# Token lists of a routed expert layer: 64 one-hot steps against four chunks of 16

## The chip, the cores and the metric

The kernel is one program on one core of a Trainium2 chip. The metric is the device time in microseconds. The engines are TensorE (matrix products, with a weight load ahead of each), VectorE, ScalarE, GpSimd (which here issues gathers and scatters by index) and SyncE (which issues plain transfers). They run side by side and meet at semaphores.

## The reference, cut to what matters

The reference is a four-layer network on 16 images of 64 channels and 16 x 16 positions, 4096 tokens. Each layer is a mixing block and a mixture of 8 experts, of which each token uses two. The change lies in the experts of the first layer:

```python
t = _to_tokens(x)                              # [16, 256, 64]: 4096 tokens
t = t + _L0_ffn_ref(_ln_t(t), L0_ffn_router_w, L0_ffn_w1, L0_ffn_w2, L0_ffn_w3)
# router -> softmax -> the best two of 8 experts, weights divided by their sum
# each expert: (silu(x @ w1) * (x @ w3)) @ w2, hidden width 682
```

This kernel computes that layer only for the experts a token has chosen: 8192 pairs of token and expert are sorted by expert, padded to whole blocks, and each block of 256 slots is computed with one expert's weights.

## The kernel before

All of it is in `routed_experts()`. A token is (partition p, turn t): p from 0 to 127, t from 0 to 31. With two choices k, a pair has the number n = 32 k + t on its partition, 0 to 63. The sort has these steps, one behind the other.

1. Preparation. The tokens are normalised (VectorE, ScalarE, and GpSimd for the power), split in a high and a low half-precision part `xs`, stored to memory as rows, turned by TensorE, and multiplied by the router's weights. Beside this ScalarE copies the ramp 0 to 127 to half precision (`iota16`, L1546), computes `row_code` = 1 + p/1024 (L1547), and the first two chunks of expert weights are split, the high half by ScalarE (`split_high`, L1449), the low half by VectorE (`split_low`, L1455).
2. Positions. VectorE finds the best two experts, counts, and gives each pair a slot. A slot is a column (0 to 77, 39 blocks of two half blocks) and a row (0 to 127): `col` and `row` (L1730, L1731).
3. Token lists. They invert the map: for slot (row r, column c), which token is it? For each n of 64, VectorE makes two one-hot arrays (L1740, L1742): `hot_slot[p, r]`, which has a code at r = row, and `hot_col[p, c]`, which has `row_code` at c = col. TensorE multiplies them (L1844) and adds all 64 in one bank. There are four buffers of each, so VectorE may be four steps ahead. As each slot has at most one pair, a sum holds one number, the product of `(1 + (n % 4) / 4) * 2 ** (n // 4)` and 1 + p/1024.
4. Owner. Three VectorE instructions (L1744 to L1747) compute which expert each of the 39 blocks belongs to.
5. Decode. 20 VectorE instructions (L1752 to L1773) take n and p out of the number's bits, and write `take` (the token's row, to be gathered) and `give` (the pair's row, to be scattered). The last raises the semaphore to LISTED.
6. GpSimd issues gathers (L1622), two for each block and seven blocks ahead, as soon as LISTED is there, and later scatters (L1630). VectorE meanwhile computes the gates (L1777 to L1788) and two low weight halves; the loads of the next weight chunks on SyncE (L1444) wait for these.
7. 39 blocks. TensorE turns the gathered rows (L1855), ScalarE copies them (L1574), TensorE multiplies (L1871), ScalarE applies Silu (L1566), VectorE multiplies (L1798, L1802), TensorE multiplies by w2 (L1881), ScalarE copies the rows out.

Each engine has its instructions in the order in which the code is written; there is no scheduler. `c.link` makes an instruction wait for the one before it on its engine. A tile's name in the profile may carry the suffix `_stage`.

## Time and profile before

| | us |
|---|---|
| device time, median of 3 runs | 1105.27 |
| lowest and highest | 1104.97, 1107.36 |
| profiled execution: first to last instruction (span) | 1104.3 |
| TensorE busy | 864.2 (78%) |
| VectorE busy | 735.0 (67%) |
| ScalarE busy | 629.9 (57%) |
| GpSimd busy | 285.6 (26%) |

Of the profiled execution the span is what is on record, with no separate device time. The busy shares are averages over stages with quite different limits. The sort and the first layer's experts lie between 117 and 410 us. A row of the timeline gives the start, the duration, the engine, the line, the operation, what it writes and reads, the number of elements per partition, and in brackets the idle time ahead of it and who ended it.

### The profile page before, as it was taken

Reading aid. Unit: us, or ns where it says so; the run is one execution under the profiler, and the core shown is the slowest. Engines: PE = TensorE matmul, PEld = TensorE weight load, DVE = VectorE, ACT = ScalarE, POOL = GpSimd, SP = SyncE. Lnnn points to the kernel's source line nnn. Section 1 sums busy time; section 2 is a strip of 40 time slices with the busy share of each in tenths; the row PEclk is TensorE's granted clock in tenths of the full one; section 3 lists DMA queues with packets and bytes.
Section 4 is the critical chain, followed back from the end, with each engine's and each line's share of the span. In section 5 each row is a group of like instructions: output and inputs, shape, how many; then the busy total and the mean of one; then the engine's idle time right before and its main releaser. Section 6 shows DMA issues by size and latency. Waiting matters only on the chain. (4 is left out here: it accounts for less than half of the span.)

```text
span 1104.3 us, 21444 instructions
## 1 busy us (share of the span) xinstructions
PE 864.2 (78%) x6822; PEld 579.7 (52%) x6822; DVE 735.0 (67%) x1964; ACT 629.9 (57%) x1293; POOL 285.6 (26%) x313
## 2 busy tenths in 40 slices
PE   4877134999999916678888867996877999958597
PEld 2665112999999915556666643443443444425232
DVE  7677788664444446878888877887585445445775
ACT  5553300654444435588888845885655777746353
POOL 3012302777777714400000002112130010025100
PEclk9889555999999966579999987997797999989699
DMA  4000271330000020101111100000100000000000
GB/s 129 1 0 0 51 132 31 93 88 20 23 22 25 19 91 1 39 30 58 38 57 38 48 20 1 1 1 21 38 1 1 1 0 0 1 12 10 1 1 38
DMA packets 25270, 32.66 MB, mean 30 GB/s; under 512 B 11582, under 2 KB 14665, under 8 KB 24814
## 3 DMA queue, kind: packets, MB, share of 16 engines
q1 hardware_dynamic: 20206, 27.50, 8.8%
q0 software_dynamic: 4992, 4.22, 1.5%
q8 instruction: 43, 0.70, 0.3%
q14 instruction: 29, 0.24, 0.1%
HBM read 19.31 MB, written 4.91 MB: 22 GB/s over the span
## 5 line engine op out<-in xcount | busy, mean ns | idle before, releaser
L1798 DVE SCALAR_TENSOR_TENSOR routed_hid_stage<-ps,routed_act_stage 128x512 f32<-128x512 f32 (+1 forms) x117 | 70.6, 604 | 100.1 <-ACT routed_act_stage L1566 98.7
L1566 ACT ACTIVATE routed_act_stage<-ps 128x512 f32<-128x512 f32 x117 | 69.9, 598 | 87.2 <-PE ps L1871 86.0
L1881 PE MATMUL ps<-w_sb,routed_hid_stage 128*128 x936 | 117.6, 269 | 0.0
L1128 ACT ACTIVATE hid_stage<-ps,b_col_sb 128x512 f32<-128x512 f32 x192 | 116.0, 698 | 0.0
L1871 PE MATMUL ps<-routed_x_stage,w_sb 128*128 128x256 f16 x858 | 114.9, 276 | 0.8 <-ACT routed_x_stage L1574 0.8
L1881 PEld LDWEIGHTS ps<-w_sb,routed_hid_stage 128*128 128x128 f32 x936 | 113.6, 192 | 1.5
L412 POOL TENSOR_TENSOR st_sb<-st_sb,neg_half_sb 128x4 f32 (+1 forms) x32 | 37.5, 1173 | 252.8 <-DVE st_sb L407 252.8
L1622 POOL DMA_INDIRECT routed_got_stage<-expert_rows,take_stage x78 | 81.6, 1047 | 78.1 <-DVE give_stage L1773 54.6
L1079 PE MATMUL ps<-x_sb,w_sb 128*128 (+1 forms) x384 | 94.5, 388 | 2.8 <-ACT hid_stage L1128 2.8
L1093 PE MATMUL ps<-hid_stage,w_sb 128*64 128x512 f32 x384 | 93.5, 606 | 1.3 <-DVE gated_stage L1160 1.3
L1871 PEld LDWEIGHTS ps<-routed_x_stage,w_sb 128*128 x858 | 84.3, 104 | 9.4 <-issue 1.1
L1160 DVE TENSOR_TENSOR gated_stage<-ps,rt_sb 128x512 f32<-128x512 f32 x64 | 44.2, 691 | 64.0 <-PE ps L1102 63.0
L1630 POOL DMA_INDIRECT expert_out<-routed_rows_stage,give_stage x78 | 79.4, 1018 | 23.8 <-issue 22.9
L322 POOL TENSOR_TENSOR st_sb<-st_sb,neg_half_sb 128x16 f32<-128x16 f32 x6 | 17.3, 2907 | 229.1 <-DVE st_sb L256 229.1
L1079 PEld LDWEIGHTS ps<-x_sb,w_sb 128*128 128x128 f16 x384 | 33.7, 99 | 76.7 <-issue 26.8
L1135 ACT ACTIVATE y_sb_stage<-ps,b_col_sb 128x512 f32<-128x512 f32 x64 | 43.4, 693 | 37.2 <-PE ps L1093 37.2
L2325 DVE CUSTOM_DVE_ANT_0 sq_sb<-ps,rel_bias_sb 128x256 f32<-128x256 f32 x128 | 47.6, 420 | 16.8 <-PE ps L2223 14.5
L1167 DVE TENSOR_TENSOR x_tok_sb<-x_tok_sb,gated_stage 128x256 f32<-128x256 f32 (+1 forms) x128 | 54.4, 425 | 5.7
L2301 ACT ACTIVATE sq_sb<-sq_sb,nmax_stage 128x256 f32<-128x256 f32 x128 | 56.0, 501 | 0.5 <-DVE nmax_stage L2325 0.3
L2325 DVE CUSTOM_DVE_ANT_0 xn_tok_sb<-ps,rel_bias_sb 128x256 f32<-128x256 f32 x128 | 47.6, 420 | 12.5 <-PE ps L2223 10.6
L2301 ACT ACTIVATE xn_tok_sb<-xn_tok_sb,nmax_stage 128x256 f32<-128x256 f32 x128 | 54.6, 500 | 0.0
L348 PE MATMUL ps<-idn_sb,xn_tok_sb 128*64 128x128 f32 x96 | 17.9, 373 | 46.8 <-DVE xn_tok_sb L264 46.8
(404 smaller groups left out, 1861.9 us busy)
## 6 DMA issues: line engine op xcount, KB each, us to landing
w_stage_sb<-f_w SPq DMA_DIRECT2D x32, 176.0 KB
x_sb<-w_sb SPq DMA_DIRECT2D x16, 256.0 KB, 2.4
rt_sb<-vals_stage SPq DMA_DIRECT2D x16, 256.0 KB, 2.3
rel_bias_sb<-bias_bands SPq DMA_DIRECT2D x16, 128.0 KB
w_stage_sb<-f_w SPq DMA_DIRECT2D x14, 128.0 KB, 3.0
w_sb<-f_w SPq DMA_DIRECT2D x1, 1536.0 KB
routed_got_stage<-expert_rows,take_stage POOLq DMA_INDIRECT x78, 2.5
expert_out<-routed_rows_stage,give_stage POOLq DMA_INDIRECT x78, 2.2
```

The source lines that it names most:

```text
L1079: last = nc.tensor.matmul(ps[:, n % BATCH, :], w16[:, part, col:col + P], xg, start=(part == 0), stop=(part == 1))
L1093: last = nc.tensor.matmul(ps[half * C:(half + 1) * C, bank, :], w2[:, at_w2:at_w2 + C], hid[:, n % RING, :], start=(m == 0), stop=(m == TP ...
L1128: nc.scalar.activation(hid[:, n % RING, :], ps[:, n % BATCH, :], func, bias=b1_col[:, b:b + 1], scale=UNSCALE).then_inc(h_act, 1)
L1167: nc.vector.tensor_tensor(xg, xg, gated[:, :, half, :], ALU.add).then_inc(added, 1)
L1566: nc.scalar.activation(act_h[:, n, :], ps[:, H1 + (q + n) % 2, :], ACT.Silu, scale=UNSCALE).then_inc(h_act, 1)
L1622: nc.gpsimd.indirect_dma_start(out=got[:, b % GOT, h, :], out_offset=None, in_=rows_d[:, :], in_offset=bass.IndirectOffsetOnAxis(ap=take[: ...
L1630: nc.gpsimd.indirect_dma_start(out=slots_d[:, :], out_offset=bass.IndirectOffsetOnAxis(ap=give[:, 2 * b + h:2 * b + h + 1], axis=0), in_=y ...
L1798: last = nc.vector.scalar_tensor_tensor(hid[:, q % 2, n, 0:full], ps[:, H3 + (q + n) % 2, 0:full], UNSCALE, act_h[:, n, 0:full], ALU.mult, ...
L1871: last = nc.tensor.matmul(o, w16[:, part, bass.ds(col, P)], xb[:, q % 2, :], start=(part == 0), stop=(part == 1))
L1881: last = nc.tensor.matmul(ps[:, Y + q % 2, h * C:(h + 1) * C], hid[:, q % 2, n, a * BLK + h * P:a * BLK + (h + 1) * P], w2[:, bass.ds(e * ...
L2301: last = nc.scalar.activation(prob[k % RING][:, a, :], prob[k % RING][:, a, :], ACT.Exp, bias=nmax[:, k % RING, a:a + 1], scale=-1.0)
L2325: last = nc.vector.tensor_tensor_reduce(out=prob[k % RING][:, a, :], in0=ps[:, k % SB, a * N:(a + 1) * N], in1=rel_bias[:, nt, hp + 4 * a, ...
```

## The change

The pairs are handled in four chunks of 16 instead of one by one.

- `iota16` now has each number of the ramp 16 times side by side, 2048 elements (L1553 of the changed kernel). `row_code` is gone; `turn16` holds n + 1 in half precision (L1554). Column and row are written in half precision, which adds one conversion (L1742) ahead of the lists.
- For a chunk VectorE compares the whole ramp with 16 columns at once (L1755, 78 x 16 = 1248 elements, equality, no code), then with 16 rows (L1757, 128 x 16 = 2048), and multiplies the column flags by n + 1 (L1760, 1248). ScalarE multiplies the column flags by the partition's number p (L1568).
- TensorE's 64 products (L1848) have 156 columns: 78 for the sum of p and 78 for the sum of n + 1. Each reads its operands at a step of 16 elements, since the 16 pairs of a chunk lie innermost. The buffers are two deep and lie in tiles that are free at that time (`sq`, `routed_act`, `routed_hid`).
- The decode needs no bits taken apart: 7 instructions in place of 20 (L1765 to L1771). The three owner instructions stand behind it (L1773 to L1776), and TensorE waits for them before the first block's turn; GpSimd waits for the decode as before.
- Some loads in this and later stages share counters (`const`, `maps`).

```diff
-            iota16 = sbl("sort_iota16", [P, P], F16)
+            LIST_CHUNKS = 4
+            PER_CHUNK = TOPK * NT // LIST_CHUNKS
+            iota16 = sbl("sort_iota16", [P, P, PER_CHUNK], F16)
+            turn16 = sbl("sort_turn16", [P, TOPK * NT], F16)
+            row16 = sbl("sort_row16", [P, TOPK * NT], F16)
+            col16 = sbl("sort_col16", [P, TOPK * NT], F16)
...
-            hot_slot = sbl("hot_slot", [P, 4, P], F16)
-            hot_col = sbl("hot_col", [P, 4, COLS0], F16)
-            row_code = sbl("sort_row_code", [P, 1])
...
+            hot_slot = sq[:, :, :].rearrange("p t c -> p (t c)").bitcast(F16).rearrange(
+                "p (q r n) -> p q r n", q=2, n=PER_CHUNK)
+            hot_col = act_h[:, :, :].rearrange("p n c -> p (n c)").bitcast(F16)[:, 0:2 * COLS0 * PER_CHUNK].rearrange(
+                "p (q c n) -> p q c n", q=2, n=PER_CHUNK)
+            coded = hid[:, :, :, :].rearrange("p q n c -> p q (n c)").bitcast(F16)[:, :, 0:2 * COLS0 * PER_CHUNK].rearrange(
+                "p q (w c n) -> p q w c n", w=2, n=PER_CHUNK)
...
-            LOW, SHIFTED, COUNTED, PLACED, OWNED, LISTED = 0, 3, 4, 5, 6, 7
+            LOW, SHIFTED, COUNTED, PLACED, LISTED, OWNED = 0, 3, 4, 5, 6, 7
...
-                    load(sp, "sort", consts[:, :], sort_d)
+                    load(sp, "const", consts[:, :], sort_d)
...
-                    act.wait_ge(loaded["sort"], want["sort"])
-                    nc.scalar.copy(iota16[:, :], iota)
-                    nc.scalar.activation(row_code[:, :], pcol, ACT.Copy, scale=1.0 / 1024, bias=1.0).then_inc(s_prepared, 1)
+                    act.wait_ge(loaded["const"], want["const"])
+                    nc.scalar.copy(iota16[:, :, :], iota.unsqueeze(2).broadcast_to((P, P, PER_CHUNK)))
+                    nc.scalar.activation(turn16[:, :], iota[:, 0:TOPK * NT], ACT.Copy, bias=1.0).then_inc(s_prepared, 1)
...
+                    for n in range(LIST_CHUNKS):
+                        act.wait_ge(s_hot, n + 1)
+                        nc.scalar.activation(coded[:, n % 2, 0, :, :], hot_col[:, n % 2, :, :], ACT.Copy,
+                                             scale=pcol).then_inc(coded_row, 1)
...
-                    nc.vector.scalar_tensor_tensor(row, col, -float(P), slot, ALU.mult, ALU.add).then_inc(s_routing, 1)
+                    nc.vector.tensor_copy(col16[:, :].rearrange("p (k t) -> p k t", k=TOPK), col)
+                    nc.vector.scalar_tensor_tensor(row16[:, :].rearrange("p (k t) -> p k t", k=TOPK), col, -float(P), slot,
+                                                   ALU.mult, ALU.add).then_inc(s_routing, 1)
...
-                    for n in range(TOPK * NT):
-                        if n >= 4:
-                            dve.wait_ge(s_products, FOUND + n - 3)
-                        k, t = n // NT, n % NT
-                        code = (1.0 + n % 4 / 4) * 2.0 ** (n // 4)
-                        nc.vector.tensor_scalar(hot_slot[:, n % 4, :], iota16[:, :], row[:, k, t:t + 1], code,
-                                                ALU.is_equal, ALU.mult)
-                        nc.vector.tensor_scalar(hot_col[:, n % 4, :], iota16[:, 0:COLS0], col[:, k, t:t + 1],
-                                                row_code[:, 0:1], ALU.is_equal, ALU.mult).then_inc(s_hot, 1)
...
-                    c.link(nc.vector.tensor_copy(flat, ps[:, LIST, 0:COLS0]))
-                    bits = flat.bitcast(mybir.dt.int32)
-                    c.link(nc.vector.tensor_scalar(fraction, bits, 0x7FFFFF, 0x3F800000, ALU.bitwise_and, ALU.bitwise_or))
-                    c.link(nc.vector.tensor_scalar(power, bits, 23, None, ALU.logical_shift_right))
...
-                    c.link(nc.vector.reciprocal(part, part))
-                    c.link(nc.vector.tensor_tensor(part, part, fraction, ALU.mult))
-                    c.link(nc.vector.tensor_scalar(part, part, 1024.0, -1024.0, ALU.mult, ALU.add))
...
-                    c.link(nc.vector.tensor_scalar(n1, power, 4.0, -508.0, ALU.mult, ALU.add))
-                    c.link(nc.vector.tensor_tensor(n1, n1, quarter, ALU.add))
-                    c.link(nc.vector.scalar_tensor_tensor(flat, part, float(NT), n1, ALU.mult, ALU.add))
+
+                    def of_chunk(v, n, rows):
+                        return v[:, n * PER_CHUNK:(n + 1) * PER_CHUNK].unsqueeze(1).broadcast_to((P, rows, PER_CHUNK))
+
+                    for n in range(LIST_CHUNKS):
+                        if n >= 2:
+                            dve.wait_ge(s_products, FOUND + n - 1)
+                        nc.vector.tensor_tensor(hot_col[:, n % 2, :, :], iota16[:, 0:COLS0, :], of_chunk(col16, n, COLS0),
+                                                ALU.is_equal).then_inc(s_hot, 1)
+                        nc.vector.tensor_tensor(hot_slot[:, n % 2, :, :], iota16[:, :, :], of_chunk(row16, n, P),
+                                                ALU.is_equal)
+                        dve.wait_ge(s_hot, n + 1)
+                        nc.vector.tensor_tensor(coded[:, n % 2, 1, :, :], hot_col[:, n % 2, :, :], of_chunk(turn16, n, COLS0),
+                                                ALU.mult).then_inc(coded_turn, 1)
+
+                    dve.wait_ge(s_products, FOUND + LIST_CHUNKS)
+                    n1, flat, second, free = (found[:, n, :] for n in range(4))
+                    c.link(nc.vector.tensor_scalar(n1, ps[:, LIST, COLS0:2 * COLS0], -1.0, None, ALU.add))
+                    c.link(nc.vector.scalar_tensor_tensor(flat, ps[:, LIST, 0:COLS0], float(NT), n1, ALU.mult, ALU.add))
...
+                    c.link(nc.vector.tensor_tensor(ends[:, :, :], iota[0:1, 0:NB].unsqueeze(2).broadcast_to((1, NB, E - 1)),
+                                                   last_[0:1, 0:E - 1].unsqueeze(1).broadcast_to((1, NB, E - 1)), ALU.is_ge))
+                    c.link(nc.vector.tensor_reduce(owner_f[:, :], ends[:, :, :], AX.X, ALU.add))
+                    nc.vector.tensor_copy(owner[:, :], owner_f[:, :]).then_inc(s_routing, 1)
...
-                    for n in range(TOPK * NT):
-                        pe.wait_ge(s_hot, n + 1)
-                        nc.tensor.matmul(ps[:, LIST, 0:COLS0], hot_slot[:, n % 4, :], hot_col[:, n % 4, :],
-                                         start=(n == 0), stop=(n == TOPK * NT - 1)).then_inc(s_products, 1)
-                    pe.wait_ge(s_routing, LISTED)
+                    for n in range(LIST_CHUNKS):
+                        pe.wait_ge(coded_row, n + 1)
+                        pe.wait_ge(coded_turn, n + 1)
+                        for m in range(PER_CHUNK):
+                            last = nc.tensor.matmul(ps[:, LIST, 0:2 * COLS0], hot_slot[:, n % 2, :, m],
+                                                    coded[:, n % 2, :, :, m].rearrange("p w c -> p (w c)"),
+                                                    start=(n + m == 0), stop=(n * PER_CHUNK + m == TOPK * NT - 1))
+                        last.then_inc(s_products, 1)
+                    pe.wait_ge(s_routing, OWNED)
 
                     def turn(b, q):
```

VectorE at the start of the lists, before: the last two position instructions, then the first steps (`sort_iota` is the ramp, `sort_pos` holds column and row).

```order
L1730 TENSOR_SCALAR sort_pos_stage<-sort_pos_stage 128x64
L1731 SCALAR_TENSOR_TENSOR sort_pos_stage<-sort_pos_stage 128x64
L1740 TENSOR_SCALAR hot_slot_stage<-sort_iota_stage,sort_pos_stage 128x128
L1742 TENSOR_SCALAR hot_col_stage<-sort_iota_stage,sort_pos_stage,sort_row_code_stage 128x78
L1740 TENSOR_SCALAR hot_slot_stage<-sort_iota_stage,sort_pos_stage 128x128
```

The same place now.

```order
L1741 TENSOR_SCALAR sort_pos_stage<-sort_pos_stage 128x64
L1742 CAST sort_col_stage<-sort_pos_stage 128x64
L1743 SCALAR_TENSOR_TENSOR sort_row_stage<-sort_pos_stage 128x64
L1755 TENSOR_TENSOR routed_act_stage<-sort_iota_stage,sort_col_stage 128x1248
L1757 TENSOR_TENSOR sq_sb<-sort_iota_stage,sort_row_stage 128x2048
L1760 TENSOR_TENSOR routed_hid_stage<-routed_act_stage,sort_turn_stage 128x1248
```

The pair of short instructions that stood 64 times has become three long ones, four times; a conversion has come in ahead.

VectorE at the end of the lists, before: the last one-hot, the owners (`sort_ends`, `owner`), and the head of the decode (`sort_found`).

```order
L1742 TENSOR_SCALAR hot_col_stage<-sort_iota_stage,sort_pos_stage,sort_row_code_stage 128x78
L1744 TENSOR_TENSOR sort_ends_stage<-sort_consts_stage,sort_blocks_stage 1x273
L1746 TENSOR_REDUCE owner_f_stage<-sort_ends_stage 1x39
L1747 CAST owner_stage<-owner_f_stage 1x39
L1752 COPY sort_found_stage<-ps 128x78
L1754 TENSOR_SCALAR sort_found_bits_stage<-sort_found_stage 128x78
L1755 TENSOR_SCALAR sort_found_bits_stage<-sort_found_stage 128x78
L1757 TENSOR_SCALAR sort_found_stage<-sort_found_bits_stage 128x78
L1758 TENSOR_SCALAR sort_found_stage<-sort_found_stage 128x78
```

The same place now, to the first instruction of the gates.

```order
L1760 TENSOR_TENSOR routed_hid_stage<-routed_act_stage,sort_turn_stage 128x1248
L1765 TENSOR_SCALAR sort_found_stage<-ps 128x78
L1766 SCALAR_TENSOR_TENSOR sort_found_stage<-ps,sort_found_stage 128x78
L1767 TENSOR_SCALAR sort_found_stage<-sort_found_stage 128x78
L1768 TENSOR_SCALAR sort_found_stage<-sort_found_stage 128x78
L1769 TENSOR_TENSOR sort_found_stage<-sort_found_stage 128x78
L1770 SCALAR_TENSOR_TENSOR take_stage<-sort_found_stage 128x78
L1771 SCALAR_TENSOR_TENSOR give_stage<-sort_found_stage 128x78
L1773 TENSOR_TENSOR sort_ends_stage<-sort_consts_stage,sort_blocks_stage 1x273
L1775 TENSOR_REDUCE owner_f_stage<-sort_ends_stage 1x39
L1776 CAST owner_stage<-owner_f_stage 1x39
L1779 TENSOR_TENSOR rt_sb<-rt_sb 128x256
```

The decode starts straight behind the last chunk and is short; the owners have moved behind `give`.

ScalarE from the squares of the preparation to the first block, before.

```order
L1544 ACTIVATE sq_sb<-xn_tok_sb 128x1024 x2
L1546 CAST sort_iota_stage<-sort_consts_stage 128x128
L1547 ACTIVATE sort_row_code_stage<-sort_consts_stage 128x1
L1449 ACTIVATE w_sb<-w_stage_sb 128x704 x2
L1552 ACTIVATE xs_tok_stage<-xn_tok_sb 128x16x64 x2
L1556 COPY x_sb<-ps 128x1024 x2
L1558 ACTIVATE rt_sb<-rt_sb 128x256
L1449 ACTIVATE w_sb<-w_stage_sb 128x704 x2
L1574 COPY routed_x_stage<-ps 128x256
```

The same stretch now.

```order
L1551 ACTIVATE sq_sb<-xn_tok_sb 128x1024 x2
L1553 CAST sort_iota_stage<-sort_consts_stage 128x2048
L1554 ACTIVATE sort_turn_stage<-sort_consts_stage 128x64
L1449 ACTIVATE w_sb<-w_stage_sb 128x704 x2
L1559 ACTIVATE xs_tok_stage<-xn_tok_sb 128x16x64 x2
L1563 COPY x_sb<-ps 128x1024 x2
L1565 ACTIVATE rt_sb<-rt_sb 128x256
L1568 ACTIVATE routed_hid_stage<-routed_act_stage,sort_consts_stage 128x1248 x4
L1449 ACTIVATE w_sb<-w_stage_sb 128x704 x2
L1585 COPY routed_x_stage<-ps 128x256
```

The ramp has grown from 128 to 2048 elements ahead of the weight splits, and four multiplications stand between the exponential and the next two splits.

## Rows read from the trace of the kernel before

**Rows 1.** The profile's page: span, and TensorE's busy time and share.
```profile
span 1104.3 us, 21444 instructions
...
PE 864.2 (78%) x6822; PEld 579.7 (52%) x6822; DVE 735.0 (67%) x1964; ACT 629.9 (57%) x1293; POOL 285.6 (26%) x313
```

**Rows 2.** Timeline (start us, us, engine, line) where the lists begin.
```profile
153.41 0.22 DVE L1731 SCALAR_TENSOR_TENSOR sort_pos_stage<-sort_pos_stage 128x64 f32<-128x64 f32 x1
153.67 0.25 DVE L1740 TENSOR_SCALAR hot_slot_stage<-sort_iota_stage,sort_pos_stage 128x128 f16<-128x128 f16 x1
153.83 0.30 DVE L1742 TENSOR_SCALAR hot_col_stage<-sort_iota_stage,sort_pos_stage,sort_row_code_stage 128x78 f16<-128x78 f16 x1
```

**Rows 3.** Groups (times, busy us, mean ns, idle before), 132 to 200 us.
```profile
L1742 DVE TENSOR_SCALAR hot_col_stage<-sort_iota_stage,sort_pos_stage,sort_row_code_stage 128x78 f16<-128x78 f16 x64 | 19.2, 300 | 0.0
L1844 PE MATMUL ps<-hot_col_stage,hot_slot_stage 128*128 128x78 f16 x64 | 15.8, 246 | 13.6 <-DVE hot_col_stage L1742 5.6
L1740 DVE TENSOR_SCALAR hot_slot_stage<-sort_iota_stage,sort_pos_stage 128x128 f16<-128x128 f16 x64 | 15.7, 246 | 0.0
...
L1827 PEld LDWEIGHTS ps<-idn_sb,xs_tok_stage 128*128 128x128 f16 x32 | 3.3, 148 | 23.2 <-DVE xs_tok_stage L1669 23.2
...
L1703 DVE TENSOR_TENSOR sort_count_stage<-sort_count_stage 128x256 f32<-128x256 f32 x5 | 2.1, 424 | 0.2
...
L1673 DVE COPY x_sb<-ps 128x1024 f16<-128x1024 f16 x2 | 1.4, 692 | 1.8 <-PE ps L1827 1.8
```

**Rows 4.** Timeline from the last one-hot step to the first gather.
```profile
177.36 0.29 DVE L1742 TENSOR_SCALAR hot_col_stage<-sort_iota_stage,sort_pos_stage,sort_row_code_stage 128x78 f16<-128x78 f16 x1
...
178.59 0.22 DVE L1752 COPY sort_found_stage<-ps 128x78 f32<-128x78 f32 x1
...
182.43 0.24 DVE L1768 SCALAR_TENSOR_TENSOR sort_found_stage<-sort_found_stage 128x78 f32<-128x78 f32 x1
...
184.94 1.39 POOL L1622 DMA_INDIRECT routed_got_stage<-expert_rows,take_stage  x1 [54.58 <-DVE give_stage L1773]
```

**Rows 5.** Busy us by stretch: TensorE, loads, VectorE, ScalarE, GpSimd; clock, DMA.
```profile
132.00:137.00 5.00, 3.59 (x32) 3.33 (x32) 3.21 (x4) 2.74 (x3) 0.00 (x0) 0.53 0.15 19
158.00:166.00 8.00, 5.34 (x22) 2.21 (x22) 8.00 (x45) 0.82 (x2) 0.00 (x0) 0.50 0.00 0
195.00:200.00 5.00, 5.00 (x49) 4.63 (x48) 3.29 (x6) 2.87 (x6) 4.05 (x4) 1.00 0.38 98
```

**Rows 6.** Groups of ScalarE, 117 to 200 us.
```profile
L1544 ACT ACTIVATE sq_sb<-xn_tok_sb 128x1024 f32<-128x1024 f32 x2 | 2.1, 1058 | 8.3 <-DVE xn_tok_sb L1655 8.3
...
L1558 ACT ACTIVATE rt_sb<-rt_sb 128x256 f32<-128x256 f32 x1 | 0.4, 417 | 3.8 <-DVE rt_sb L1684 3.8
```

**Rows 7.** Timeline of the preparation, 124 to 131 us.
```profile
124.19 0.28 ACT L1546 CAST sort_iota_stage<-sort_consts_stage 128x128 f16<-128x128 f32 x1
...
124.48 1.45 ACT L1449 ACTIVATE w_sb<-w_stage_sb 128x704 f16<-128x704 f32 x2
...
125.77 0.88 DVE L1455 SCALAR_TENSOR_TENSOR w_sb<-w_stage_sb,w_sb 128x704 f16<-128x704 f32 x1
127.54 1.23 DVE L1665 TENSOR_TENSOR xn_tok_sb<-xn_tok_sb,st_sb 128x1024 f32<-128x1024 f32 x1 [0.89 <-POOL st_sb L1611]
...
130.40 1.23 DVE L1665 TENSOR_TENSOR xn_tok_sb<-xn_tok_sb,st_sb 128x1024 f32<-128x1024 f32 x1 [0.83 <-POOL st_sb L1611]
```

**Rows 8.** Timeline around the first block, 188 to 193 us.
```profile
188.09 1.70 DVE L1455 SCALAR_TENSOR_TENSOR w_sb<-w_stage_sb,w_sb 128x704 f16<-128x704 f32 x2
189.00 2.38 SPq L1444 DMA_DIRECT2D w_stage_sb<-f_w  x4
...
192.86 0.69 DVE L1798 SCALAR_TENSOR_TENSOR routed_hid_stage<-ps,routed_act_stage 128x512 f32<-128x512 f32 x1 [3.08 <-ACT routed_act_stage L1566]
192.87 0.79 ACT L1449 ACTIVATE w_sb<-w_stage_sb 128x704 f16<-128x704 f32 x1
```

**Rows 9.** The dearest product per column, by form, whole span.
```profile
L335 PE MATMUL ps<-rel_bias_sb 3*32 3x512 f32 x2 | 1.9, 1056 | 6.3 <-DMA rel_bias_sb<-l_m 6.3
```

More of the change, by code:

```diff
@@ L158, in metaformer @@
         pool_chain = Chain(sem("pool_chain"))
-        loaded = {k: sem(f"loaded_{k}") for k in ("x", "const", "sort", "l0", "f", "l1", "l2", "l3", "bias")}
+        loaded = {k: sem(f"loaded_{k}") for k in ("x", "const", "l0", "f", "l1", "maps", "bias")}
         want = dict.fromkeys(loaded, 0)
@@ L1487, in routed_experts @@
             y_row = sbl("routed_rows", [P, 4, 2 * C])
+            hot_slot = sq[:, :, :].rearrange("p t c -> p (t c)").bitcast(F16).rearrange(
[4 more added lines that the diff above has]
+                "p q (w c n) -> p q w c n", w=2, n=PER_CHUNK)
             CH = 3
-            names = ("copied", "routing", "products", "prepared", "hot",
+            names = ("copied", "routing", "products", "prepared", "hot", "coded_row", "coded_turn",
                      "rows_stored", "x_turned", "x_copied", "setup", "rows_by_act")
-            (s_copied, s_routing, s_products, s_prepared, s_hot,
+            (s_copied, s_routing, s_products, s_prepared, s_hot, coded_row, coded_turn,
              s_stored, x_turned, x_copied, s_setup, rows_by_act) = (sem(f"routed_{n}") for n in names)
@@ L1721, in _ @@
                     c.link(nc.vector.tensor_tensor(rest, ranked, base.unsqueeze(1).broadcast_to((P, NT, E)), ALU.add))
-                    slot, raw, col, row = (pos[:, n, :, :] for n in range(4))
+                    slot, raw, col = (pos[:, n, :, :] for n in range(3))
                     for k, hot in enumerate((hot1, hot2)):
@@ L1744, in _ @@
-                    c.link(nc.vector.tensor_tensor(ends[:, :, :], iota[0:1, 0:NB].unsqueeze(2).broadcast_to((1, NB, E - 1)),
-                                                   last_[0:1, 0:E - 1].unsqueeze(1).broadcast_to((1, NB, E - 1)), ALU.is_ge))
-                    c.link(nc.vector.tensor_reduce(owner_f[:, :], ends[:, :, :], AX.X, ALU.add))
-                    nc.vector.tensor_copy(owner[:, :], owner_f[:, :]).then_inc(s_routing, 1)
-                    dve.wait_ge(s_products, FOUND + TOPK * NT)
@@ L1750, in _ @@
-                    n1, flat, second, free, quarter, part = (found[:, n, :] for n in range(6))
-                    power, fraction = found_bits[:, 0, :], found_bits[:, 1, :]
-                    c.link(nc.vector.tensor_copy(flat, ps[:, LIST, 0:COLS0]))
-                    bits = flat.bitcast(mybir.dt.int32)
-                    c.link(nc.vector.tensor_scalar(fraction, bits, 0x7FFFFF, 0x3F800000, ALU.bitwise_and, ALU.bitwise_or))
-                    c.link(nc.vector.tensor_scalar(power, bits, 23, None, ALU.logical_shift_right))
@@ L1756, in _ @@
-                    fraction = fraction.bitcast(F32)
-                    c.link(nc.vector.tensor_scalar(quarter, fraction, 4.0, -4.45, ALU.mult, ALU.add))
-                    c.link(nc.vector.tensor_scalar(quarter, quarter, 12582912.0, None, ALU.add))
-                    c.link(nc.vector.tensor_scalar(quarter, quarter, 12582912.0, None, ALU.subtract))
-                    c.link(nc.vector.tensor_scalar(part, quarter, 0.25, 1.0, ALU.mult, ALU.add))
-                    c.link(nc.vector.reciprocal(part, part))
@@ L1762, in _ @@
-                    c.link(nc.vector.tensor_tensor(part, part, fraction, ALU.mult))
-                    c.link(nc.vector.tensor_scalar(part, part, 1024.0, -1024.0, ALU.mult, ALU.add))
-                    c.link(nc.vector.tensor_scalar(part, part, 12582912.0, None, ALU.add))
-                    c.link(nc.vector.tensor_scalar(part, part, 12582912.0, None, ALU.subtract))
-                    c.link(nc.vector.tensor_scalar(n1, power, 4.0, -508.0, ALU.mult, ALU.add))
-                    c.link(nc.vector.tensor_tensor(n1, n1, quarter, ALU.add))
@@ L2382, in _ @@
                 def _(sp):
-                    load(sp, "l2", map_w[:, :], L2)
+                    load(sp, "maps", map_w[:, :], L2)
                     load_small(sp, F2)
@@ L2514, in _ @@
                     inverse(0)
-                    pe.wait_ge(loaded["l2"], want["l2"])
+                    pe.wait_ge(loaded["maps"], want["maps"])
                     mapped(0)
@@ L2632, in _ @@
                 def _(sp):
-                    load(sp, "l3", cw[:, :, :], L3)
+                    load(sp, "maps", cw[:, :, :], L3)
                     load_small(sp, F3)
```

9 lines of the change are left out of this document (4 added, 5 removed).

## The prediction

> **What bounds the kernel now.** The busiest engine, TensorE, is at work 78% of a span of 1104.3 us [rows 1], so no engine sets the time as a whole; each stage has its own chain. I went first to the order of time around the sort (the function the diff touches), then to the groups of instructions of that stretch, then to the table of busy time by stretch, and last to the waits of GpSimd. The reader is to see one serial chain. GpSimd's first gather of token rows waits 54.58 us, for the token lists' last VectorE instruction [rows 4]. TensorE has nothing else in that time: it is at its lower clock, 0.50 of full speed, 1.2 GHz [rows 5], and ScalarE is nearly idle [rows 5]. So each microsecond by which the first gather comes earlier should come off the whole time, if the 39 expert blocks behind it run at the same pace; they run on TensorE, busy throughout from 195 us [rows 5], and nothing in them is touched.
>
> The chain from the last position instruction to the first gather has three pieces.
> - The 64 one-hot steps: the first starts at 153.67 [rows 2], the last pair's second half at 177.36 [rows 4]. From 153.83 to 177.36 are 63 steps, 0.3735 us each, though the two instructions of a step last 0.246 and 0.300 [rows 3]: two instructions without a wait between them overlap by (0.546 - 0.3735) / 2 = 0.086 us each. VectorE is busy all of this time; TensorE's 64 products of 0.246 us fit inside.
> - Three small instructions on the owner of each block, up to the decode's first instruction at 178.59.
> - The decode, 20 instructions, 178.59 to the gather at 184.94 [rows 4].
>
> **What the change does to VectorE's lists.** Each of four chunks now issues three two-source instructions in half precision: 1248, 2048 and 1248 elements per partition. No row of before shows a two-source instruction with half-precision inputs, so I bound it. In single precision with two sources 1024 elements last 1.23 us [rows 7] and 256 last 0.424 [rows 3]: 1.05 ns per element on a fixed 0.155. A half-precision copy of 1024 lasts 0.692 [rows 3]: with that fixed part, 0.524 ns per element, twice the pace. Slow end, 1.05 ns: 1.465 + 2.305 + 1.465 = 5.24, less three overlaps of 0.086, 4.98 us a chunk. At 0.524 ns: 0.81 + 1.23 + 0.81 = 2.85, less 0.26, 2.6 us a chunk. A fast end, at 0.262 ns, isn't excluded by anything in these rows: 1.65 less 0.26, 1.4 us a chunk. I take 2.6: the copy is the one row in which all operands are two bytes wide and lie side by side, as here (the broadcast list repeats rows of 16 neighbours). Four chunks: 10.4 us.
>
> Which pace the chip takes is stated in the Trainium skill, Vector Engine (DVE) Microarchitecture Reference, section 5.1: a two-source instruction runs at two elements per cycle if all operands have two bytes and an innermost step of one, a row read again and again included, and never at four. By it the chunk is 2.6 us and the fast end drops out; without it the single-precision rows would have been as near, and the sum 9.5 us worse. No row here shows the case.
>
> **ScalarE's part of a chunk.** It multiplies the 1248 column flags by the partition's number, when the first VectorE instruction of the chunk is done. 1024 elements last 1.058 us and 256 last 0.417 [rows 6]: 0.835 ns per element on 0.203, so 1.25 us. It starts 0.81 into the chunk and ends at 2.1, before VectorE's third instruction ends at 2.6. Cost nothing; the cover is VectorE's second and third instruction. Behind it ScalarE has two weight splits, needed only at the end of the gates; slack of several us.
>
> **TensorE's part.** Still 64 products, now with 156 columns instead of 78, in bursts of 16 at the end of a chunk, and both operands read at a step of 16 elements (32 bytes). The nearest row in clock and kind is the 32 turnings at 0.53 of full clock, 128 columns of half precision, 3.59 us [rows 5]: 0.112 each with its weight load, so 0.137 for 156 columns, if the step costs nothing. A burst is 2.2 us, under the chunk's 2.6, so three bursts hide behind VectorE's next chunk and only the last one stands on the path. The two-deep buffers hold: chunk n waits for burst n-2, over by then. Low end 0.08 if the clock had risen (0.9 us less in the last burst); high ends are the rivals below. I take 0.137, the nearest row; that a step costs nothing at 1.2 GHz, where a column is asked for half as often as at full clock, is an assumption.
>
> **The sum to the first gather.** A conversion of the columns to half precision is added before the lists, about 0.15 us (the instruction before the lists lasts 0.22 with 64 elements [rows 2], less an overlap): first chunk at 153.8. Lists on VectorE until 153.8 + 10.4 + 0.1 = 164.3. Last burst 2.2, with 0.2 for the hand-over and the end of the last product: 166.7. The owner instructions, 1.07 us, have gone behind the decode. Of the decode remain seven instructions: one at 0.26, then the six that stand from 182.43 to the gather at 184.94, 2.51 us [rows 4]. First gather at 166.7 + 0.26 + 2.5 = 169.5, against 184.94: **15.4 us less**.
>
> **What lies beside it.** (a) The ramp of 16 copies of each number is a ScalarE copy of 2048 elements in place of 128: 0.203 + 2048 x 0.835 ns = 1.9 us, against 0.28, from 124.3 [rows 7]. Both splits of weights move by 1.6 us, the first to 126.3 to 127.1. VectorE's matching half moves from 125.77 to 127.1 and ends at 128.0, and holds up the first scaling (127.54) by 0.5 us; the second scaling waits for GpSimd until 130.40 [rows 7], and only behind it goes the chain on. Cost zero; with that cover gone, 0.5. (b) The three owner instructions now stand before the gates and the two low weight halves. In before these end at 189.79 and VectorE's first product comes at 192.86 [rows 8]: 3.07 us of slack for 1.07. TensorE needs the owners only when the first rows have been gathered, 4 us behind the decode. But the loads that SyncE issues behind the low halves (189.00) start 1.07 later in relation to the blocks, and ScalarE takes their first chunk at 192.87 [rows 8]. I cost this at zero; bounds 0 and 1.1 us, once. (c) The gather, the Silu table load and the first blocks come as one piece. (d) Loads share counters now; each is waited for in full long after it was issued: zero.
>
> The sum stands against the profiled span of 1104.3; the runs' median is 1105.27, 0.97 more, which I leave in place. 1105.27 - 15.4 = **1089.9 us**.
>
> **Rivals.**
> 1. *Two-source half precision runs at one element per cycle.* VectorE's chunk is 4.98 us, all four 19.9 instead of 10.4: 5.9 us saved, 1099.4. For it: every two-source row of before has the slow pace. Against: all of those have a four-byte operand.
> 2. *TensorE pays for the step in its operands.* If loads no longer hide behind the product before, a product costs 0.148 [rows 3] + 0.137 = 0.285 us; a burst is 4.6, longer than a chunk, and TensorE becomes the bound: 153.8 + 2.7 + 64 x 0.285 = 174.7, decode and hand-over 2.9, gather at 177.6: 7.3 us saved, 1098.0. For it: no product of before has a step in its operands. Against: the array is at half clock. The Trainium skill has a rule that speaks for it: Advanced Engine Details and Errata, section SBUF Cachelines, says that reads need at least two hits in a 16-byte line to keep full pace; with a step of 32 bytes there is one. No row here shows it.
> 3. *Slower than before:* the same step, dearer. The dearest product per column in before is 1.9 us for two of 512 columns [rows 9], 1.86 ns a column. If all 156 columns and 128 weights cost that, a product is 0.53 us and the 64 take 33.8: gather at 193.3, 8.3 us later, 1113.6. It decides from the price p at which 153.8 + 2.7 + 64 p + 2.9 = 184.94, p = 0.40 us a product. Against: three times what the rows at this clock give.
>
> **How the numbers follow.** Forecast 0.66, rival 2 0.15, rival 1 0.12, rival 3 0.04, and 0.03 for no measurable change (a product near 0.40, or blocks that give it back). Of a run of this kernel some 0.2%, 2.2 us, can be told from nothing. Rivals 1 and 2 are faster too: faster 0.93, same 0.03, slower 0.04. Range: the low end is the fast VectorE bound, in which TensorE's 64 products at 0.137 set the lists (gather at 167.0, 1087.4), with a few tenths for the first blocks; the high end takes in rival 2 and leaves out rival 1. 1087.0 to 1098.5.
>
> **What would show it.** The three new VectorE instructions at 0.81, 1.23 and 0.81 us (slow: 1.46, 2.30, 1.46); gaps on VectorE only after the fourth chunk, not before the third; TensorE in four bursts of about 2.2 us with idle time between; ScalarE's 1.25 us inside; the first gather at 169.5; the first Silu and the last scatter both earlier by the same 15 us. Wrong if VectorE waits for products before chunk 3, or if the blocks begin 15 us earlier but end less than that earlier.

## The result and the profile after

| | before | changed |
|---|---|---|
| device time, median of 5 runs | 1105.23 | 1099.55 |
| lowest and highest | 1103.97, 1107.36 | 1096.77, 1101.78 |
| ratio to before, 95% interval | | 0.9951 [0.9932, 0.9971] |
| span of the profiled execution | 1104.3 | 1097.8 |

The kernel is faster by 5.4 us (0.9951 of 1105.23; by the interval 3.2 to 7.5), where 15.4 were forecast. 1099.55 lies above the range of 1087.0 to 1098.5.

The page of the changed kernel, to be held against [rows 1]:

```profile
span 1097.8 us, 21323 instructions
...
PE 862.9 (79%) x6822; PEld 579.3 (53%) x6822; DVE 718.5 (65%) x1836; ACT 636.9 (58%) x1297; POOL 286.4 (26%) x313
```

The timeline of the lists to the first gather, to be held against [rows 2, 4]. L1755, L1757 and L1760 are VectorE's three instructions of a chunk, L1568 ScalarE's, L1848 the products.

```profile
155.49 0.20 DVE L1742 CAST sort_col_stage<-sort_pos_stage 128x64 f16<-128x64 f32 x1
...
155.86 0.81 DVE L1755 TENSOR_TENSOR routed_act_stage<-sort_iota_stage,sort_col_stage 128x1248 f16<-128x1248 f16 x1
156.58 1.22 DVE L1757 TENSOR_TENSOR sq_sb<-sort_iota_stage,sort_row_stage 128x2048 f16<-128x2048 f16 x1
156.70 1.33 ACT L1568 ACTIVATE routed_hid_stage<-routed_act_stage,sort_consts_stage 128x1248 f16<-128x1248 f16 x1 [13.84 <-DVE routed_act_stage L1755]
157.72 0.80 DVE L1760 TENSOR_TENSOR routed_hid_stage<-routed_act_stage,sort_turn_stage 128x1248 f16<-128x1248 f16 x1
...
158.66 18.60 PE L1848 MATMUL ps<-routed_hid_stage,sq_sb 128*128 128x156 f16 x64 [7.97 <-DVE routed_hid_stage L1760]
...
163.47 0.81 DVE L1755 TENSOR_TENSOR routed_act_stage<-sort_iota_stage,sort_col_stage 128x1248 f16<-128x1248 f16 x1 [2.38 <-PE ps L1848]
...
168.07 0.81 DVE L1755 TENSOR_TENSOR routed_act_stage<-sort_iota_stage,sort_col_stage 128x1248 f16<-128x1248 f16 x1 [1.94 <-PE ps L1848]
...
177.30 0.24 DVE L1765 TENSOR_SCALAR sort_found_stage<-ps 128x78 f32<-128x78 f32 x1 [6.56 <-PE ps L1848]
...
180.09 1.48 POOL L1633 DMA_INDIRECT routed_got_stage<-expert_rows,take_stage  x1 [47.64 <-DVE give_stage L1771]
```

Three things stand in it. VectorE's instructions last 0.81, 1.22 and 0.80 us, as taken, and ScalarE's 1.33. But VectorE waits 2.38 us before the third chunk, 1.94 before the fourth, and 6.56 for the last burst. And the 64 products run without a gap for 18.60 us: 0.291 us each instead of 0.137, or 0.288 from start to start. The stretch from the first list instruction to the first gather is 180.09 - 155.86 = 24.23 us, against 184.94 - 153.67 = 31.27: 7.04 less, not 15.4.

The products by themselves: duration in ns (smallest, middle, largest), then the start of the first and last. One product lasts 469 ns though the next starts 288 ns behind it, so products overlap; what counts is the pace, 18.60 / 64.

```profile
L1848 PE MATMUL ps<-routed_hid_stage,sq_sb x64: 461/469/477, 158.7 to 176.8; 128*128 128x156 f16 x64
```

The table by stretch (columns as in [rows 5]): TensorE is at work all the time, still at the granted clock 0.50.

```profile
158.00:166.00 8.00, 7.34 (x26) 3.87 (x27) 5.62 (x7) 2.71 (x3) 0.00 (x0) 0.50 0.11 27
166.00:177.00 11.00, 11.00 (x40) 5.46 (x37) 2.80 (x4) 2.70 (x3) 0.00 (x0) 0.50 0.00 0
```

Behind the first gather something is given back. From it to the stage's last loads (SyncE, 390.76) are 210.67 us, against 209.63 before (394.57 - 184.94). ScalarE in the first block shows a wait that was not there in [rows 8], for the fifth chunk of weights:

```profile
187.71 0.60 ACT L1577 ACTIVATE routed_act_stage<-ps 128x512 f32<-128x512 f32 x1 [1.08 <-PE ps L1877]
189.20 0.79 ACT L1449 ACTIVATE w_sb<-w_stage_sb 128x704 f16<-128x704 f32 x1 [0.89 <-DMA w_stage_sb<-f_w]
```

The preparation, to be held against [rows 7]: the ramp is the row of 1.88 us, VectorE's first weight half has slid to 128.80, the first scaling now follows it without a wait, and the second scaling still follows GpSimd's powers (the row of 5.97 us, both of them).

```profile
126.05 1.88 ACT L1553 CAST sort_iota_stage<-sort_consts_stage 128x2048 f16<-128x2048 f32 x1
...
126.47 5.97 POOL L1622 TENSOR_TENSOR st_sb<-st_sb,neg_half_sb 128x16 f32<-128x16 f32 x2 [4.09 <-DVE st_sb L1671]
...
128.80 0.89 DVE L1455 SCALAR_TENSOR_TENSOR w_sb<-w_stage_sb,w_sb 128x704 f16<-128x704 f32 x1 [1.08 <-ACT w_sb L1449]
129.61 1.23 DVE L1676 TENSOR_TENSOR xn_tok_sb<-xn_tok_sb,st_sb 128x1024 f32<-128x1024 f32 x1
...
132.48 1.23 DVE L1676 TENSOR_TENSOR xn_tok_sb<-xn_tok_sb,st_sb 128x1024 f32<-128x1024 f32 x1 [0.83 <-POOL st_sb L1622]
```

From the stage's first load to the first list instruction: 155.86 - 119.36 = 36.50 us, against 153.67 - 117.49 = 36.18. These 0.3 us are the new conversion (0.11 from start to start) and GpSimd's powers, 5.97 in place of 5.75. The 0.2 of the powers goes with the long ramp: in every profile with 16 copies they take 5.97, and in those with 4, 2 or 1 copies 5.75, as in before.

The stage as a whole: 390.76 - 119.36 = 271.40 against 277.08, 5.7 us less: 7.04 - 1.04 - 0.32. The runs' 5.4 us agrees with it. The two profiled spans differ by 6.5: behind the last loads the changed one needs 2.8 us less (707.0 against 709.8), and its stage begins 1.9 later. That stretch behind the stage lies between 706.6 and 712.2 us over the profiles of the changed versions, whose code is the same there, so neither is taken for a gain. Where the stage begins (117.5 to 121.3 us over the profiles of this study, with nothing changed ahead of it) says nothing of the change.

### The profile page after: what moved, and what is told of

It is laid out like the page before. It is cut to its first block and busy times, and to the rows that moved or that the text cites. A ratio compares the mean times of both kernels' runs of the same rounds, so it can differ in the third digit from the quotient of the medians.

```text
span 1097.8 us, 21323 instructions
## 1 busy us (share of the span) xinstructions
PE 862.9 (79%) x6822; PEld 579.3 (53%) x6822; DVE 718.5 (65%) x1836; ACT 636.9 (58%) x1297; POOL 286.4 (26%) x313
## 5 line engine op out<-in xcount | busy, mean ns | idle before, releaser
L1887 PE MATMUL ps<-w_sb,routed_hid_stage 128*128 x936 | 117.5, 269 | 0.0
L2312 ACT COPY w_stage_sb<-ps 128x512 f32<-128x512 f32 x64 | 37.5, 586 | 30.0 <-PE ps L2251 29.9
```

Of the source, the lines that this page charges most:

```text
L1887: last = nc.tensor.matmul(ps[:, Y + q % 2, h * C:(h + 1) * C], hid[:, q % 2, n, a * BLK + h * P:a * BLK + (h + 1) * P], w2[:, bass.ds(e * ...
```

## The experiments

All compare three stretches in the trace: a product (TensorE's busy time of the 64, over 64), the lists (first list instruction to first gather), and the stage (first load to last loads). The busy time has the end of each burst in it; where the pace from start to start inside a burst is meant, the text says so. Versions for which no time is given ran once, for their profile.

The layout of the lists got two parameters, the number of pairs that lie innermost. SUB_W is for the weights (`hot_slot`, 128 columns, loaded ahead of each product), SUB_M for the moving operand (`coded`, the 156 columns that the product goes through). The pairs of a chunk then lie in 16 / SUB groups, and TensorE reads at a step of SUB elements. The changed kernel is SUB 16. VectorE and ScalarE write the same numbers of elements in the new order.

```diff
+            SUB_W, SUB_M = 4, 4
...
-                "p (q c n) -> p q c n", q=2, n=PER_CHUNK)
+                "p (q g c s) -> p q g c s", q=2, c=COLS0, s=SUB_M)
...
-                            last = nc.tensor.matmul(ps[:, LIST, 0:2 * COLS0], hot_slot[:, n % 2, :, m],
-                                                    coded[:, n % 2, :, :, m].rearrange("p w c -> p (w c)"),
+                            last = nc.tensor.matmul(ps[:, LIST, 0:2 * COLS0], hot_slot[:, n % 2, m // SUB_W, :, m % SUB_W],
+                                                    coded[:, n % 2, m // SUB_M, :, :, m % SUB_M].rearrange("p w c -> p (w c)"),
```

**Both operands at a step of 4** (SUB_W = SUB_M = 4).

> The changed kernel with the 16 pairs of a chunk laid out as four groups of four: both operands of the 64 list products are read at a step of 4 elements (8 bytes) instead of 16 (32 bytes); columns, product count and VectorE's instructions stay. Theory A (the step of the operands is what makes a product last 0.29 us): a product 0.13 to 0.15 us, each burst about 2.2 us, VectorE no longer waits before the third and fourth chunk, first list instruction to first gather 15.5 to 17 us instead of 24.2, whole time 7 to 9 us under the changed kernel. Rival B (156 columns at the low clock cost 0.29 us whatever the step): a product stays at 0.29, the lists at 24.2 us, no change. Rival C (both operands short of one per line matter only partly): in between.

Measured, group of the products (count, busy us, mean ns) and timeline:

```profile
L1854 PE MATMUL ps<-routed_hid_stage,sq_sb 128*128 128x156 f16 x64 | 9.7, 321 | 8.5 <-DVE routed_hid_stage L1766 8.2
```
```profile
154.07 0.81 DVE L1761 TENSOR_TENSOR routed_act_stage<-sort_iota_stage,sort_col_stage 128x1248 f16<-128x1248 f16 x1
...
156.88 5.00 PE L1854 MATMUL ps<-routed_hid_stage,sq_sb 128*128 128x156 f16 x32 [7.97 <-DVE routed_hid_stage L1766]
...
159.35 0.81 DVE L1761 TENSOR_TENSOR routed_act_stage<-sort_iota_stage,sort_col_stage 128x1248 f16<-128x1248 f16 x1
...
161.93 0.80 DVE L1761 TENSOR_TENSOR routed_act_stage<-sort_iota_stage,sort_col_stage 128x1248 f16<-128x1248 f16 x1
162.16 5.01 PE L1854 MATMUL ps<-routed_hid_stage,sq_sb 128*128 128x156 f16 x32 [0.28 <-DVE routed_hid_stage L1766]
...
169.99 1.48 POOL L1634 DMA_INDIRECT routed_got_stage<-expert_rows,take_stage  x1 [39.33 <-DVE give_stage L1777]
```

A product 0.152 us, VectorE's third chunk follows at its own pace, the lists 15.92 us, the stage 380.34 - 117.58 = 262.76. Time 1094.46, ratio 0.9901 [0.9879, 0.9924]. Theory A holds, rival B (it is the 156 columns) falls: their number is the same.

Each PE row holds two bursts. The granted clock was 0.50 until 161.19, at the end of the second burst, and 1.00 from there to behind the last, and the two rows are alike: a product starts 0.142 us behind the one before it at either level, against 0.288 in the changed kernel.

The runs gained less than the stage shows (10.9 us, 8.4 to 13.4 by the interval, against 14.3). In the profile the loss lies behind the stage, in the stretch that differs from profile to profile: 712.2 us here, the longest of all. Why the four runs come out so is open; the version with a short ramp and the owners in the wait, below, shows no such loss in its runs.

**Only the moving operand at 4** (SUB_W = 16, SUB_M = 4).

> Only the moving operand (156 columns) at a step of 4 elements, the weights (128) still at 16. If the moving operand's step is the price: a product at 0.13 to 0.16 us. If the weights' step is: 0.29 stays. If both: between, and the two single changes each give a part.

```profile
L1854 PE MATMUL ps<-routed_hid_stage,sq_sb 128*128 128x156 f16 x64 | 10.0, 326 | 8.4 <-DVE routed_hid_stage L1766 8.3
```

**Only the weights at 4** (SUB_W = 4, SUB_M = 16).

> Only the weights at a step of 4 elements, the moving operand still at 16. If the moving operand's step is the price: 0.29 us a product stays. If the weights' step is: 0.13 to 0.16 us.

```profile
L1854 PE MATMUL ps<-routed_hid_stage,sq_sb 128*128 128x156 f16 x64 | 18.3, 463 | 8.0 <-DVE routed_hid_stage L1766 8.0
```

With the moving operand changed a product is at 0.156 and the lists at 16.06; with the weights alone at 0.286 and 23.92. The price is the moving operand's: 0.135 us of the 0.139. The weights' step costs 0.004 to 0.005. From start to start it is the same picture: 0.288 for both at 16, 0.283 with the weights at 4, 0.147 with the moving operand at 4, 0.142 with both.

**Owners ahead of the decode**, in VectorE's wait for the last burst.

```diff
+                    c.link(nc.vector.tensor_tensor(ends[:, :, :], iota[0:1, 0:NB].unsqueeze(2).broadcast_to((1, NB, E - 1)),
+                                                   last_[0:1, 0:E - 1].unsqueeze(1).broadcast_to((1, NB, E - 1)), ALU.is_ge))
+                    c.link(nc.vector.tensor_reduce(owner_f[:, :], ends[:, :, :], AX.X, ALU.add))
+                    nc.vector.tensor_copy(owner[:, :], owner_f[:, :]).then_inc(s_routing, 1)
                     dve.wait_ge(s_products, FOUND + LIST_CHUNKS)
```

> The changed kernel with the three owner instructions moved ahead of the decode, into the time in which VectorE waits 6.6 us for the last burst. Theory (the owners' 1.07 us behind the decode make the loads of the fifth weight chunk late for ScalarE, 0.89 us): the wait of ScalarE's first split in the blocks goes from 0.89 to under 0.1 us, first gather unchanged in relation to the lists, time from first gather to the last scatters' end 0.5 to 1 us shorter. Rival (the blocks' 1.0 us longer time is clock and chance): no change there, time the same within a few tenths.

```profile
188.32 0.60 ACT L1577 ACTIVATE routed_act_stage<-ps 128x512 f32<-128x512 f32 x1 [1.04 <-PE ps L1878]
188.96 0.79 ACT L1449 ACTIVATE w_sb<-w_stage_sb 128x704 f16<-128x704 f32 x1
```

The wait for weights is gone, and from the first gather (180.96) to the last loads (390.66) are 209.70 us, as in before (209.63). So what was given back was the owners'. The expectation's rival, the clock, falls: it rose 10.2 us behind the first gather here and 10.1 in the changed kernel. In size the effect is less sharp than one pair says: over all profiles the stretch takes 210.2 to 210.7 us with the owners behind the decode and 209.3 to 209.7 with them ahead, so 0.5 to 1.0 over before. In the runs it can't be seen: 1100.07, ratio 0.994 [0.9917, 0.9963], which overlaps the changed kernel's.

**Both operands at 8.**

> The changed kernel with two groups of eight in a chunk: both operands at a step of 8 elements (16 bytes). Theory A1 (a column costs by the 16-byte line it opens, as the Trainium skill has it in Advanced Engine Details and Errata, SBUF Cachelines): each column is then a line of its own, as at step 16, and a product costs 0.29 us. Theory A2 (the cost grows with the distance step by step): a product between 0.15 and 0.29, about 0.2 us. VectorE's three instructions stay at 0.81, 1.22 and 0.80.

The 64 products in one row:

```profile
159.28 18.21 PE L1854 MATMUL ps<-routed_hid_stage,sq_sb 128*128 128x156 f16 x64 [7.97 <-DVE routed_hid_stage L1766]
```

0.285 us each, the lists 180.32 - 156.47 = 23.85. Half the distance costs the same, as A1 (by the line that a column opens) has it, and A2 does not.

**Both operands at 2.**

> The changed kernel with eight groups of two in a chunk: both operands at a step of 2 elements (4 bytes), and a broadcast of two neighbours on VectorE. Theory A: a product 0.13 to 0.14 us at the granted clock 0.50 and 0.07 to 0.09 at 1.00, where the step of 4 had 0.13 at either clock; lists to first gather 15 to 15.9 us. If VectorE's pace needs longer runs of neighbours, its instructions go to 1.46, 2.30, 1.46 us and the lists to about 25 us.

A product is 0.140 us (2.24 for 16; 0.130 from start to start), as expected at clock 0.50, but the lists are at 20.61, since VectorE has slowed down in the two instructions that read the ramp, and not in the third:

```profile
L1763 DVE TENSOR_TENSOR sq_sb<-sort_iota_stage,sort_row_stage 128x2048 f16<-128x2048 f16 x4 | 8.1, 2014 | 0.0
L1761 DVE TENSOR_TENSOR routed_act_stage<-sort_iota_stage,sort_col_stage 128x1248 f16<-128x1248 f16 x4 | 5.2, 1292 | 0.0
L1766 DVE TENSOR_TENSOR routed_hid_stage<-routed_act_stage,sort_turn_stage 128x1248 f16<-128x1248 f16 x4 | 3.3, 815 | 0.0
```

**Columns alone.** Extra products in TensorE's idle time.

```diff
+                    def columns(step, copies):
+                        return ps[:, LIST, 0:2 * COLS0], x16[:, 0:P], x16[:, 0:2 * COLS0 * step:step], copies
...
+                    o, w, m, reps = columns(16, 48)
+                    for _i in range(reps):
+                        nc.tensor.matmul(o, w, m, start=True, stop=True)
```

> The changed kernel with extra products at the start of TensorE's part of the stage, while it would be idle: 160 products of 156 columns side by side as a warm-up, then 48 each at a column step of 1, 2, 4, 8 and 16 elements (half precision, weights side by side), then 48 with the weights at a step of 16. Their results are not used. If a column costs by the line it opens: 0.065 to 0.07 us at full clock at step 1, 2 and perhaps 4, then 0.29 at 8 and 16. If the price is only there at the low clock: 16 costs 0.15 at full clock. If a wide step costs in proportion: 0.07, 0.07, 0.13, 0.2, 0.29. Weights at a step of 16: the same as step 1 within 0.01.

48 products at a step of 1, 2, 4, 8 and 16, one row each, then 48 with the weights at 16 and the columns side by side:

```profile
133.07 3.40 PE L1833 MATMUL ps<-x_sb 128*128 128x156 f16 x48
136.31 3.52 PE L1836 MATMUL ps<-x_sb 128*128 128x156 f16 x48
139.67 6.88 PE L1839 MATMUL ps<-x_sb 128*128 128x156 f16 x48
146.37 13.46 PE L1842 MATMUL ps<-x_sb 128*128 128x156 f16 x48
159.65 13.75 PE L1845 MATMUL ps<-x_sb 128*128 128x156 f16 x48
173.22 5.03 PE L1849 MATMUL ps<-x_sb 128*128 128x156 f16 x48
```

By the starts, over 48: 0.0675 us at a step of 1, 0.070 at 2, 0.140 at 4, 0.277 at 8, 0.283 at 16. The clock of these stretches (step 1, step 4, step 8 in its two parts, step 16):

```profile
133.07:136.31 3.24, 3.24 (x52) 3.24 (x50) 2.98 (x3) 1.06 (x1) 0.00 (x0) 1.00 0.19 22
139.67:146.37 6.70, 6.70 (x52) 5.55 (x49) 0.00 (x0) 0.00 (x0) 0.00 (x0) 1.00 1.12 137
146.37:149.25 2.88, 2.88 (x13) 1.28 (x11) 0.00 (x0) 0.00 (x0) 0.00 (x0) 1.00 1.14 141
149.35:159.65 10.30, 10.30 (x38) 4.66 (x37) 0.00 (x0) 0.00 (x0) 0.00 (x0) 0.50 0.87 211
159.65:172.50 12.85, 12.85 (x47) 5.85 (x46) 0.00 (x0) 0.00 (x0) 0.00 (x0) 0.50 0.00 0
```

Product by product, the pace at a step of 8 is 0.277 us before the clock falls at 149.29 and 0.277 behind it. With only the weights stepped it is 0.130 while the clock is 0.50 and 0.068 at 1.00; the first products of the warm-up, with nothing stepped, have 0.130 and 0.0675. So the weights' step costs nothing that can be seen here. In the stretch of step 16 no other engine works and no transfer runs, so nothing else competes for the memory while a product takes 0.283.

What fits is a price for each 16-byte line that a product opens. A step of 8 or 16 opens 156 lines for 156 columns, 1.8 ns a line (1.85 in the changed kernel); a step of 4 opens 78, again 1.8 ns, at either clock (0.142 in the lists, 0.140 here). A step of 2 opens 39, which at that price is 0.070 us, no more than the columns need anyway (0.0675, or 0.43 ns each, at full clock), so there the two can't be told apart. At 0.50 the columns need 0.130 us, so there a step of 4 was nearly free. That a line is 16 bytes wide, and not eight elements, no run shows: all of them read half precision.

The rule cited in rival 2 (the Trainium skill, Advanced Engine Details and Errata, SBUF Cachelines) is right in kind: one column a line is slow. It asks for at least two hits in a line for full pace. A step of 4 has two, and at full clock they are not enough, 0.140 against 0.0675; at the lower clock they nearly are, 0.142 against 0.130.

**Step 4, short ramp, owners in the wait** (the version that the runs pointed to).

```diff
-            iota16 = sbl("sort_iota16", [P, P, PER_CHUNK], F16)
+            iota16 = sbl("sort_iota16", [P, P, 4], F16)
```

The owners' three instructions stand where the experiment on them had put them.

> The version the runs so far point to: step of 4 in both operands, the ramp with 4 copies instead of 16, and the owners ahead of the decode, in VectorE's wait for the last burst. Expected: lists to first gather 15.9 us, ScalarE's wait for the fifth weight chunk gone, first gather to the stage's last loads 209.7 instead of 210.3; 13 to 15 us under the kernel before, about 1090 to 1092. If the whole time gives back more than that (as it did with the step of 4 alone: 14.2 us at the stage's end, 10.9 in the runs' ratio), it stays at 1093 to 1095, and the loss lies in the later stages.

```profile
164.99 0.42 DVE L1769 TENSOR_TENSOR sort_ends_stage<-sort_consts_stage,sort_blocks_stage 1x273 f32<-1x273 f32 x1
...
165.91 0.17 DVE L1772 CAST owner_stage<-owner_f_stage 1x39 int32<-1x39 f32 x1
167.69 0.24 DVE L1776 TENSOR_SCALAR sort_found_stage<-ps 128x78 f32<-128x78 f32 x1 [1.61 <-PE ps L1855]
...
170.47 1.39 POOL L1634 DMA_INDIRECT routed_got_stage<-expert_rows,take_stage  x1 [39.43 <-DVE give_stage L1782]
```

The owners (164.99 to 166.08) lie in front of the decode, and VectorE still waits 1.6 us. Lists 170.47 - 154.56 = 15.91, from there to the last loads 209.44, stage 261.72: 15.4 less than before, as much as the prediction had forecast for the changed kernel. Time 1088.13, ratio 0.9841 [0.9813, 0.987]: 17.6 us less (14.4 to 20.7). This beats both kernels.

**Step 2 with a ramp of 2.**

> As the version with step 4, ramp and owners (four copies), but at a step of 2 with a ramp of 2 copies side by side, so that VectorE's first operand is read without gaps (with a ramp of 16 copies it read 2 of each 16 and went to 1.27 and 1.99 us). Theory (VectorE lost pace by the gaps in the ramp): 0.81, 1.22, 0.80 again, a product 0.14 at the granted clock 0.50 or 0.07 at 1.00, lists to first gather 15.0 to 15.9 us, whole time 0 to 1 us under the step of 4. Rival (rows of two neighbours are themselves slow in a two-source instruction): 1.27 and 1.99 stay, the lists at 20.6 us, 4 to 5 us over the step of 4.

VectorE is back at 0.81, 1.22 and 0.80, so the gaps in the ramp had cost it, not the short rows. The bursts:

```profile
159.89 2.24 PE L1855 MATMUL ps<-routed_hid_stage,sq_sb 128*128 128x156 f16 x16 [7.97 <-DVE routed_hid_stage L1766]
162.46 2.11 PE L1855 MATMUL ps<-routed_hid_stage,sq_sb 128*128 128x156 f16 x16 [0.33 <-DVE routed_hid_stage L1766]
165.04 1.29 PE L1855 MATMUL ps<-routed_hid_stage,sq_sb 128*128 128x156 f16 x16 [0.46 <-DVE routed_hid_stage L1766]
167.61 2.18 PE L1855 MATMUL ps<-routed_hid_stage,sq_sb 128*128 128x156 f16 x16 [1.28 <-DVE routed_hid_stage L1766]
```

One burst came at full clock (1.29), three did not. Lists 172.61 - 157.08 = 15.53, stage 261.20. Time 1089.83, ratio 0.9858 [0.9832, 0.9883]: not to be told from the step of 4.

**Step 1.**

> The same lists with both operands of the products side by side (step 1), the ramp in one copy: the broadcast operand of VectorE is then one element read again for all columns. TensorE: 0.14 us a product, as at step 2. VectorE: if two elements per cycle need the innermost step of one in every operand, 1.46, 2.30 and 1.46 us, and the lists 4 x 4.97 + 2.4 + 3 = 25 us to the first gather; if not, 0.81, 1.22, 0.80 and 15.9 us.

```profile
L1763 DVE TENSOR_TENSOR sq_sb<-sort_iota_stage,sort_row_stage 128x2048 f16<-128x2048 f16 x4 | 9.1, 2284 | 0.0
L1761 DVE TENSOR_TENSOR routed_act_stage<-sort_iota_stage,sort_col_stage 128x1248 f16<-128x1248 f16 x4 | 5.8, 1454 | 0.0
L1766 DVE TENSOR_TENSOR routed_hid_stage<-routed_act_stage,sort_turn_stage 128x1248 f16<-128x1248 f16 x4 | 5.8, 1451 | 0.0
```

TensorE's burst stays at 2.24 us; VectorE's instructions last 1.45, 2.28 and 1.45 us, and the lists take 179.35 - 154.29 = 25.06. This was rival 1's price (1.46, 2.30, 1.46), seen at last, where one operand is a single element read again.

## Why the prediction was wrong

- *What bounds the kernel:* right. In every version of the lists the stage moved with the time of the first gather, apart from the preparation's 0.3 us and the 1.0 of the weights.
- *VectorE's lists:* right. Forecast 0.81, 1.23, 0.81 and 2.6 us a chunk; measured 0.81, 1.22, 0.80, start to start 155.86 to 158.44 = 2.58. The unseen operation was priced by the row whose operands have the same width and lie as closely. The traces agree with the rule that the prediction cites for it (the Trainium skill, Vector Engine (DVE) Microarchitecture Reference, section 5.1): 2048 elements take 1.22 us with rows of 16, 4 and 2 neighbours read again. With a single element read again they take 2.28.
- *ScalarE's part:* 1.33 against 1.25, hidden.
- *TensorE's part:* **this is the step that failed.** "I take 0.137 ... that a step costs nothing at 1.2 GHz ... is an assumption." The step cost 0.154 us a product: 0.291 in place of 0.137. The rest of the term was sound, for at steps of 1 and 2 a product took 0.130 to 0.140 at the same clock. The burst is 4.65 us, longer than the chunk, so the products set the lists: 2.80 (first chunk) + 18.6 + 2.8 (decode and hand-over) = 24.2, against 15.7 forecast. At a step of 4 the forecast's arithmetic came out: 15.9.
- *The number was rival 2's,* 0.285 a product and 7.3 us; measured 0.291 and 7.0. Its sum took the price from loads that no longer hide, and the weights' step costs 0.005 at most, so its figure was right by luck. The rule on lines that it names beside the sum is the one that the runs bear out, for the moving operand. And the whole time, 1099.55, is nearest to rival 1's 1099.4, which is chance too: VectorE ran at the forecast pace.
- *The decode:* seven instructions and the way to GpSimd took 177.30 to 180.09, 2.79 against 2.77.
- *Beside it:* the ramp, costed at zero with 0.5 as its bound (a), cost 0.2. The owners' shift was costed at zero with a bound of 1.1 us (b); it cost 1.04 in this profile, and 0.5 to 1.0 over all of them. The load had been issued 3.87 us before its use; the slack was never checked with a row that shows it landing.
- *The range:* rival 2 was taken in at 1098.0 with 0.5 us above it. With the owners' 1.1 it would have been 1099.1, and with the ramp's 0.5 too 1099.6, against 1099.55 measured. Two terms that the text had bounded were not added at the range's high end.

## What to carry to other kernels

When a loop is turned inside out so that one engine gets long instructions, look at what the new layout does to the reader: for TensorE's moving operand count the 16-byte lines that a product opens, at about 1.8 ns each (half precision, as measured here), and compare with its columns at the clock of that stretch. Often there is a layout between the two (here groups of four) that leaves the writer's instructions as they are and gives the reader several columns a line. And if a bound is written down for a small term, add it at the end of the range, above all beside a rival that is already near it.
